# First attention in six slots a block instead of seven: row maxima in three fillings of 500 columns

## The reference

```
x = x + L0_xattn(layernorm(x), ctx, ctx)   # 16 heads of 16, softmax over the 375, output projection
x = x + L0_ffn(layernorm(x))               # 8 experts, top 1, 112 tokens at most each, 256 -> 1024 -> 256
x = x + L1_xattn(layernorm(x), ctx, ctx)   # one head of 256, no output projection
x = x + L1_ffn(layernorm(x))               # 256 -> 1024 -> 256, gelu, with a low-rank part from tokens 1 to 16
```

## Time and profile before

| | us |
|---|---|
| runs of the kernel before | 373.71, 375.99, 375.95 (median 375.95) |
| the profiled execution, its own time | 375.83 |
| its span, first to last instruction | 374.1 |
| around the span | 1.7 |
| busy in the span: TensorE, VectorE, ScalarE, GpSimd | 352.0, 182.4, 151.5, 57.3 |
| mean granted TensorE clock | 0.995 of full |

### The profile page before, as it was taken

The page is one execution under the profiler, slowest core; times in us unless marked ns, Lnnn a source line. Parts: engine busy times, 40 slices in busy tenths (PEclk is TensorE's granted clock), DMA queues, the critical chain, the costliest instruction groups (busy, mean ns, idle before and its releaser), DMA issues.

```text
span 374.1 us, 7931 instructions
## 1 busy us (share of the span) xinstructions
PE 352.0 (94%) x3108; PEld 265.1 (71%) x3108; DVE 182.4 (49%) x573; ACT 151.5 (40%) x361; POOL 57.3 (15%) x95
## 2 busy tenths in 40 slices
PE   3889999999999999998989999999889999999996
PEld 1545666666576656666768998998668889798875
DVE  4773344756566484746361122212489667532500
ACT  0525464555645463535523221120245667523300
POOL 2730000010101010101020000012694421200000
PEclk9999999999999999999989999999999999999999
DMA  8946060420000010006108299970110011111000
GB/s 244 348 112 226 2 224 4 171 69 2 12 4 12 2 42 3 14 12 229 58 25 259 75 348 327 299 210 25 50 48 3 3 53 52 40 39 50 26 25 25
DMA packets 24885, 35.29 MB, mean 94 GB/s; under 512 B 2608, under 2 KB 21408, under 8 KB 24736
## 3 DMA queue, kind: packets, MB, share of 16 engines
q1 hardware_dynamic: 22160, 31.73, 27.0%
q0 software_dynamic: 768, 1.84, 1.7%
q10 hardware_dynamic: 1920, 1.21, 1.2%
HBM read 31.06 MB, written 3.72 MB: 93 GB/s over the span
## 4 chain that ended last, share of the span: by engine, by line
PE 49%; DVE 3%; ACT 2%; issue 1%; DMA 1%; POOL 0%; DVEq 0%; ACTq 0%; POOLq 0%; SPq 0%
PE ps L588 8%; PE ps L733 8%; PE ps L598 7%; PE ps L711 6%; PE ps L490 4%; PE ps L664 3%; PE ps L680 2%; PE ps L654 2%; PE ps L467 1%; PE ps L365 1%; PE ps L724 1%; PE ps L741 1%; PE ps L449 1%; DMA xn<-expert_out_dram,idx_get 1%; ACT heads L847 1%
## 5 line engine op out<-in xcount | busy, mean ns | idle before, releaser
L1070 DVE TENSOR_REDUCE mneg<-ps 112x2 f32<-112x750 f32 x64 | 57.1, 934 | 47.0 <-PE ps L430 46.9
L430 PE MATMUL ps<-heads 32*112 32x375 f32 x256 | 39.3, 518 | 1.9 <-DVE mneg L1070 1.2
L847 ACT ACTIVATE heads<-ps 125x896 f32<-125x896 f32 x34 | 29.3, 915 | 12.2 <-PE ps L449 12.2
L374 PE MATMUL ps<-ctxT,w_in 128*128 128x375 f32 x64 | 26.8, 545 | 7.8 <-DMA ctxT<-in_ctxT 6.4
L1284 POOL TENSOR_TENSOR rstd<-veps,neghalf 112x1 f32<-112x1 f32 x32 | 18.4, 575 | 82.7 <-DVE veps L1036 82.6
L588 PEld LDWEIGHTS ps<-xT,ring 128*128 128x128 f32 x256 | 29.8, 192 | 1.2 <-ACT xT L801 0.7
L588 PE MATMUL ps<-xT,ring 128*128 128x112 f32 x256 | 29.9, 275 | 0.5 <-ACT xT L801 0.5
L733 PE MATMUL ps<-heads,ring 128*112 128x256 f32 x128 | 28.8, 382 | 0.0
L598 PE MATMUL ps<-ring,heads 128*112 128x256 f32 x128 | 28.8, 379 | 0.0
L430 PEld LDWEIGHTS ps<-heads 32*112 32x112 f32 x256 | 14.9, 169 | 17.6 <-issue 12.5
L449 PE MATMUL ps<-heads 32*125 32x224 f32 x384 | 26.9, 358 | 0.0
(11 more groups left out here) (143 smaller groups left out, 562.9 us busy)
## 6 DMA issues: line engine op xcount, KB each, us to landing
ring<-in_L_ffn_W SPq DMA_DIRECT2D x16, 1024.0 KB, 7.3
ctxT<-in_ctxT SPq DMA_DIRECT2D x8, 375.0 KB, 11.3
heads<-in_L_ffn_W SPq DMA_DIRECT2D x2, 1024.0 KB, 9.9
ring<-x_by_odd_rows_dram SPq DMA_DIRECT2D x4, 448.0 KB, 3.6
ring<-in_mask SPq DMA_DIRECT2D x1, 1312.5 KB, 9.1
expert_in_dram<-eo SPq DMA_DIRECT2D x1, 896.0 KB, 11.2
b2row<-in_L_ffn_b SPq DMA_DIRECT2D x8, 112.0 KB, 8.1
out_dram<-ring SPq DMA_DIRECT2D x8, 112.0 KB, 1.9
```

Of the source, the lines that this page charges most:

```text
L374: mm = pe.matmul(o[:, 0:S2], w_in[:, 1, k, m * P:(m + 1) * P], ctxT[:, k, b * S2:(b + 1) * S2], start=k == 0, stop=k == DT - 1)
L430: mm = pe.matmul(bank(j)[0:S, 0:S2], qz[rows, m, a, b * S:(b + 1) * S], kt[b % 3][rows, m, :], start=True, stop=True)
L847: act.activation(weights(b, step)[0:KC, pair.start:pair.stop, :], ps[0:KC, pair.start:pair.stop, 0:2 * QW], ACT.Exp, scale=DK ** -0.5).the ...
L1070: v.tensor_reduce(mneg[:, b % 2, PAIRS * g + pair.start:PAIRS * g + pair.stop], ps[0:S, pair.start:pair.stop, 0:S2], AX.X, ALU.max, negate ...
```

## The change

An iteration has six slots, three with scores (0, 2, 4) and three with row maxima (1, 3, 5). The sixteen heads' maxima now take three fillings of 500 columns a bank: step 0 holds group 0 whole and the first 125 keys of group 1, step 1 the other 250 keys of group 1 and the first 250 of group 2, step 2 group 3 whole and the last 125 keys of group 2 (`MAX_PARTS`). VectorE reduces 250 and 750 elements a half in steps 0 and 2 and 1000 in step 1; ND0 and ND1 first take the minimum of the two negated parts of group 1 or 2 (`mpart`). The stages move between slots: C5 from slot 6 to slot 0 of the next iteration, between NM1 and C1; K0 ahead of C6; V1 to slot 2, K1 to slot 3; V2, C4 and NM0 to slot 4; U and ND1 to slot 5, where the weighted sums are formed. QX and Q1 move to earlier slots, so that the Q projections of a pair of blocks are done an iteration before their first use. Seven chunks of context values instead of five are in slots of iterations 6 and 7, six instead of seven in front of the experts.

```
-SLOTS = 7
+SLOTS = 6
 SCORE_STEPS = 3
 SCORE_AT = {0: 0, 2: 1, 4: 2}
-MAX_AT = {1: 0, 3: 1, 5: 2, 6: 3}
+MAX_AT = {1: 0, 3: 1, 5: 2}
+MAX_PARTS = (((0, 0, 375), (1, 0, 125)), ((1, 125, 375), (2, 0, 250)), ((3, 0, 375), (2, 250, 375)))
...
 PIPE = {
-    0: [("NM1", 0), ("C1", 1), ("D5", 2), ("V0", -1)],
-    1: [("C2", 1), ("C6", 2), ("K0", -2), ("D6", 2)],
-    2: [("C3", 1)],
-    3: [("V1", -1)],
-    4: [("L2", 1), ("ND0", -1), ("K1", -2)],
-    5: [],
-    6: [("U", 0), ("NM0", -1), ("C4", 1), ("V2", -1), ("C5", 1), ("ND1", -1)],
+    0: [("NM1", 0), ("C5", 2), ("C1", 1), ("D5", 2), ("V0", -1)],
+    1: [("C2", 1), ("K0", -2), ("C6", 2), ("D6", 2)],
+    2: [("C3", 1), ("V1", -1)],
+    3: [("L2", 1), ("ND0", -1), ("K1", -2)],
+    4: [("V2", -1), ("C4", 1), ("NM0", -1)],
+    5: [("U", 0), ("ND1", -1)],
 }
...
-Q_SLOTS = {(0, 2): "QX", (0, 3): "Q0", (1, 2): "Q1"}
+Q_SLOTS = {(0, 1): "Q1", (0, 3): "Q0", (1, 3): "QX"}
...
-CTX_AT = {(6, 1): 1, (6, 4): 1, (7, 0): 1, (7, 4): 2}
-CTX_BEFORE_EXPERTS = 7
+CTX_AT = {(6, 1): 1, (6, 3): 2, (7, 0): 1, (7, 2): 1, (7, 4): 2}
+CTX_BEFORE_EXPERTS = 6
...
-    if (i % 2, u) in Q_SLOTS and i >= 0 and i // 2 + 1 < QCHUNKS:
-        yield Q_SLOTS[i % 2, u], i // 2 + 1
+    if (i, u) == (0, 0):
+        yield "QX", 1
+    if (i % 2, u) in Q_SLOTS and i >= 0 and (i + 3) // 2 < QCHUNKS:
+        yield Q_SLOTS[i % 2, u], (i + 3) // 2
...
-            def row_max(b, g):
-
-                m, a = divmod(g, 2)
-                read(("K", b, m))
-                read(("Q", b // 2, m))
-                for half, pair in HALVES:
-                    open_tiles(("MX", b, g), half)
-                    for j in pair:
-                        rows = slice(32 * j, 32 * j + 32)
-                        mm = pe.matmul(bank(j)[0:S, 0:S2], qz[rows, m, a, b * S:(b + 1) * S], kt[b % 3][rows, m, :],
-                                       start=True, stop=True)
-                    mm.then_inc(filled[half], 1)
+            def row_max(b, step):
+
+                for g, _, _ in MAX_PARTS[step]:
+                    read(("K", b, g // 2))
+                    read(("Q", b // 2, g // 2))
+                for n, (g, lo, hi) in enumerate(MAX_PARTS[step]):
+                    m, a = divmod(g, 2)
+                    at = n * (MAX_PARTS[step][0][2] - MAX_PARTS[step][0][1])
+                    for half, pair in HALVES:
+                        if n == 0:
+                            open_tiles(("MX", b, step), half)
+                        for j in pair:
+                            rows = slice(32 * j, 32 * j + 32)
+                            mm = pe.matmul(bank(j)[0:S, at:at + hi - lo], qz[rows, m, a, b * S:(b + 1) * S],
+                                           kt[b % 3][rows, m, lo:hi], start=True, stop=True)
+                        if n == 1:
+                            mm.then_inc(filled[half], 1)
...
-            def row_max(b, g):
+            def row_max(b, step):
                 for half, pair in HALVES:
-                    _, free = full(("MX", b, g, half))
-                    v.tensor_reduce(mneg[:, b % 2, PAIRS * g + pair.start:PAIRS * g + pair.stop],
-                                    ps[0:S, pair.start:pair.stop, 0:S2], AX.X, ALU.max, negate=True).then_inc(free, 1)
+                    _, free = full(("MX", b, step, half))
+                    js = slice(pair.start, pair.stop)
+                    if step == 1:
+                        top = mneg[:, b % 2, PAIRS:3 * PAIRS].rearrange("p (g j) -> p j g", j=PAIRS)[:, js, :]
+                        v.tensor_reduce(top, ps[0:S, js, 0:500].rearrange("p j (g k) -> p j g k", g=2), AX.X, ALU.max,
+                                        negate=True).then_inc(free, 1)
+                    else:
+                        top = mneg[:, b % 2, PAIRS * MAX_PARTS[step][0][0]:][:, js]
+                        v.tensor_reduce(mpart[:, step // 2, js], ps[0:S, js, 375:500], AX.X, ALU.max, negate=True)
+                        v.tensor_reduce(top, ps[0:S, js, 0:375], AX.X, ALU.max, negate=True).then_inc(free, 1)
...
                     for half, _ in HALVES:
-                        drained_by_me(("MX", b, 2 * m + 1, half))
+                        drained_by_me(("MX", b, m + 1, half))
+                    split = mneg[:, b % 2, PAIRS * (m + 1):PAIRS * (m + 2)]
+                    step(v.tensor_tensor(split, split, mpart[:, m, :], ALU.min))
...
-            wait_filled(("Q", QCHUNKS - 1, DT - 1))
+            wait_filled(("Q", QCHUNKS - 1, 0))
```

More of the change, by code:

```diff
@@ L210, in build @@
         mneg = sb("mneg", [S, 2, H])
+        mpart = sb("mpart", [S, 2, PAIRS])
         mpieces = sb("mpieces", [S, DT, 2, P], BF16)
```

## The result

| | before | after |
|---|---|---|
| median of the runs | 375.18 (4) | 380.76 (4) |
| lowest, highest | 373.71, 375.99 | 379.22, 381.64 |
| the profiled execution, its own time | 375.83 | 381.18 |
| its span | 374.1 | 379.4 |

In brackets stands the number of executions. The ratio is 1.015, with a 95% interval of 1.0119 to 1.018: the change makes the kernel slower by one and a half per cent. The forecast was 378.5, 2.6 over the median it set out from; the medians here lie 5.6 apart.

What follows compares the result with a forecast made beforehand. TensorE's waits where the four tile banks change hands, not its busy share, were taken as the bound. Terms +0.68, +1.40, +0.97, +0.55 and -0.9 summed to +2.7 on the profiled 375.83 (median 375.95): 378.5, range 375.5 to 383.0.

Steps and rivals of the forecast that it cites:

- TensorE ... then stands until 2.15: Slot 0: V0, reached 0.95 after scores0, waits until 2.15 for NM1's bank, costing 1.20 less the bank wait it swallows.
- Rival 1: No stall at V0, NM1's bank being free in time: 7.9 off, 370.6, faster; chance 0.11.
- The 0.7 that it gave to block 0: Rival 1's saving in block 0, where the second transposition of QX meets the bank wait.
- The sum for an even block: From scores0's end to the next in even blocks, with a Q projection in the first filling's slot: 21.00.
- An odd block: From scores0's end to the next: 20.93, with scores1 waiting 0.8 for VectorE's reductions.
- Block 1: The block without C5 in slot 0: V0 done at 1.51 after scores0, the block 19.33.
- the start's +0.68: First filling through block 0 to scores0's end in block 1: 49.33 for 48.65.
- granted clocks under 1 appear before 183 us: One of the signs named as showing the forecast wrong: TensorE's granted clock below full before 183 us.
- Rival 2: TensorE's clock falls with the recurring waits, up to 1.7 per fall; one gives 380.2, two 381.9; chance 0.15.
- Rival 3: The short 125-column passes are dear, F = 1.17 and more on VectorE's start: +3, 381.6; chance 0.12.
- the forecast's F: Time of a 500-column filling on TensorE that waits for nothing: 1.06, upper bound 1.17.
- The tail: From C1 of block 7 on: one context chunk fewer in front of the experts, -0.9.

Runs made afterwards that it cites:

- the second profile: The changed kernel run again unchanged, for a second profile: 381.29, ratio 1.0195.
- the edited kernel: The changed kernel with the first QX, Q1 and Q0 moved into iteration -1, stall at V0 left in: 381.21, once more 380.78.
- the kernel with the stall alone: The kernel before with only C5 moved from slot 6 to slot 0, between NM1 and C1: 383.38, ratio 1.0198.

## Why the prediction came out as it did

**The sign and the mechanism.** "TensorE ... then stands until 2.15" was right to the hundredth, in the changed kernel and in the kernel before with the one stage moved. Rival 1 (no stall) was priced 7.9 below the forecast; removing the stall took 6.9 off the time and 7.34 off the spacings. The 0.7 that it gave to block 0 does not show: from the first filling to the first copy of ctxU it took 33.99 in the second profile with the stall and 33.94 without, both with the clock at half there. Rival 1's 370.6 was still out of reach, since the loss in the start was missing from it; with that mended too, the kernel took 373.31 and 372.05.

**The block.** The sum for an even block against block 4: V0 done 3.21 (forecast 3.11), scores1 done 4.83 later (3.71 + 1.12), second filling 1.91 later (1.92), scores2 done 4.63 later (4.62), third filling and its wait 2.94 (2.96), weighted sums 2.44 (2.44), scores0 1.18 (1.12). It makes 21.14 for 21.00. An odd block was put at 20.93, since nothing but VectorE was to bound it; it measured 21.14 too, with the wait for the reductions in scores1 that was forecast, 0.68 for 0.8. Block 1 took 19.58 for 19.33: V0 is done 1.50 after scores0 there, and its first filling then waits for the high banks (it takes 1.43, 52.29 to 53.72), which by the prediction's own rule come free at 1.90; the sum left that out. Block 5 took 21.41, with 0.27 more between scores2 and the weighted sums than block 4; the reason is open. Together these small sizes are 1.22 in blocks 1 to 5 and 0.21 in block 6.

**The start, where a step failed.** The sum said "Start: from 16.76 ... scores0 of block 0 ends at 29.3", 12.54 after the first filling, and block 0 "20.1", at a full clock. Measured: 14.44 and 21.05. Of the first 1.90, 0.94 is VectorE: the third filling began 8.64 after the first instead of 7.70. But 0.72 of it is the late end of the normalisation of x in this one execution; in the second profile it was 7.92. After it the forecast's 4.8 to the end of scores0 would have held, 4.83 in the edited kernel with its full clock, but it was 5.80: the clock fell at 27.0. It stayed low until 33.8, in block 0, which took 1.0 more. So the failed step is the start's +0.68: the text saw that "nothing covers" the third filling's reductions, and left the clock out of it. The term measured +3.60, and +3.15 and +3.24 in the other two profiles. The prediction had named "granted clocks under 1 appear before 183 us" as a sign that it is wrong, and by that sign it was, at 27.0 to 33.8. The change cost about twice what was forecast; that the time still lies 2.3 from the forecast owes something to luck, since in the profile -1.46 of scatter stood against the start.

**Rival 2** had the right mechanism and the wrong place. It expected falls where V0 stands; a wait of 1.05 us in each of six blocks did not bring one, neither here nor in the kernel with the stall alone. The fall came behind the one stretch with 1.63 of 3.40 us busy. With the first Q projections in that stretch the clock stayed full through the start in all five profiles taken; with them in block 0 it fell in the start in all five profiles of kernels with six slots. Its price, "up to 1.7" for a fall of 3.4 us, stands beside the 2.2 measured for one that lasted 6.8, part of it beside other waits. The Trainium skill, TensorE: Matmul & The Clock Gate, A second HAM failure mode: psum-queue depth-cycling, says that frequent short idles between groups of matmuls make the clock swing as PSUM banks are cycled. The recurring waits of these traces did not, six of 1.05 us among them with a full clock for the whole span; the fall in the start came behind waits for VectorE that are there once (1.50 and 0.77).

**Rival 3** is out: a free filling of 500 columns takes 1.04 to 1.06 (115.86 to 116.91), the forecast's F, not 1.17. The 125-column passes cost their columns, and no bare weight load shows in them, which would make it 1.17.

**The tail** gained 1.17 for 0.9, from one context chunk fewer (six in 6.32 us), with the fall that the earlier trace rows show now at 197.7 instead of 192.1.

**The total.** Forecast +2.7, measured +5.37: start 1.46 (2.92 less the scatter), blocks 1 to 5 1.22, block 6 0.21, block 7 0.05, tail -0.27.

The best version here has the three fillings, NM1 at the end of its slot and the first Q projections in iteration -1: 372.05, ratio 0.9918 [0.9889, 0.9947]; with one reduction for two it is the same within the scatter.

## What to carry to other kernels

Where small results go round a few banks, moving or adding one opening changes the partner of each later one: list for every opening the one that frees its bank, and the queue in which that drain stands. A change that makes one engine's steps longer must be followed through the prologue too, where nothing covers them; a single hole there can cost the clock for microseconds after it, here about 2 us. And a test of one part in the old order (the fillings alone, +7 to +8 us) says little on a change whose gain needs both parts.

## What the runs showed of the hardware

The granted clock did not go by the number of waits: six of 1.05 us for one copy, one every 21.9 us, left it full for the whole span. In the start, 6.8 us at 0.50 came behind 1.63 and 1.33 of 3.40 us busy (changed kernel, and the one without the stall), and it stayed full behind 2.21, 2.07 and 2.85. Busy time alone does not tell, though: 2.14 of 3.40 stood ahead of the fall in the earlier trace rows, and of that at 197.7 in the changed kernel. In the second profile of the changed kernel the clock fell at 269.2 for 3.4 us behind a stretch that counts as busy for all of its 3.40 us, 20 of its 28 matmul records one column wide; behind the same work in the second run of the version with the early Q projections (257.70 to 261.10) it stayed full. VectorE's maximum over PSUM takes 413 ns for 250 elements a partition, 928 for 750 and 1196 for 1000 in fp32. By the first two an element is 1.03 ns and an instruction 155 ns beside its elements; one instruction for two saves 146 (1341 less 1195). The fall of 3.4 us at 269.2 cost nothing that shows (173.05 from the first expert matmul to the end, for 173.1 without); beside the one of 6.8 us in the run with one reduction stood 0.9 more, in one profile.
